# An AdaLN block of attention and a LoRA feed-forward layer: inputs turned on the host, LayerNorm on columns, the shift as a bias, and an instruction order of its own for each engine

## What is computed

```python
mod = (silu(c) @ wmod).reshape(B, 6, 1, H)           # c: 4 x 1024, wmod: 1024 x 6144
sa, ca, ga, sb, cb, gb = (mod[:, i] for i in range(6))
ga = (2 * (ga >= 0) - 1) * maximum(abs(ga), 0.25)     # gb the same
h = layernorm(x) * (1 + ca) + sa
q, k, v = split(h @ Wqkv + bqkv)                      # Wqkv: 1024 x 768
x = x + ga * (softmax(q @ k.T / 16) @ v @ Wo + bo)
h = layernorm(x) * (1 + cb) + sb
lora = (h @ A[adapter].T) @ Bw[adapter].T             # rank 16, an adapter for each batch, or none
x = x + gb * (h @ weight.T + bias + lora)             # weight: 1024 x 1024
```

## Time and profile before

| | |
|---|---|
| median of 3 runs | 1152.91 us (1152.84 to 1154.0) |
| the profiled execution's own time | 1153.4 us |
| its span, first to last instruction | 1151.6 us |
| mean granted clock of the matrix engine | 0.976 of full |
| busy, share of the span | PE 94%, PEld 78%, DVE 55%, ACT 33%, POOL 21% |
| moved by DMA | 160.26 MB, 139 GB/s over the span |

### The profile page before, as it was taken

How to read it: one execution, slowest core, us unless ns; L and a number is a source line. 1 busy time by engine, 2 the same in 40 slices (tenths; PEclk the granted TensorE clock), 3 DMA queues, 4 the chain that set the end, 5 groups by cost and what they waited for, 6 DMA issues and landing times.

```text
span 1151.6 us, 13779 instructions
## 1 busy us (share of the span) xinstructions
PE 1084.6 (94%) x5593; PEld 895.4 (78%) x5593; DVE 632.7 (55%) x837; ACT 381.0 (33%) x630; POOL 241.9 (21%) x211
## 2 busy tenths in 40 slices
PE   7799998999999999989999997999989999999996
PEld 2576997888987889878889875788777877787775
DVE  1830256463455462565625658737767776677631
ACT  0831144241343231542315443403422332323310
POOL 1000011231111221021401233233134122324122
PEclk9799999999998999999999998999999999999998
DMA  9975201533014340124310678543525462454221
GB/s 326 374 271 198 77 1 47 194 124 112 1 37 147 115 178 1 38 92 164 135 48 19 178 276 290 183 164 110 202 80 194 145 202 75 163 201 164 97 86 55
DMA packets 51968, 160.26 MB, mean 139 GB/s; under 512 B 5217, under 2 KB 9729, under 8 KB 51905
## 3 DMA queue, kind: packets, MB, share of 16 engines
q1 hardware_dynamic: 42208, 125.01, 31.4%
q0 software_dynamic: 9696, 34.36, 7.9%
HBM read 121.60 MB, written 37.75 MB: 138 GB/s over the span
## 4 chain that ended last, share of the span: by engine, by line
PE 64%; DVE 12%; issue 9%; DMA 6%; ACT 5%; POOL 3%; SPq 0%; DVEq 0%; POOLq 0%; ACTq 0%
PE pairA L1106 5%; PE pairB L1106 5%; PE pairA L1107 5%; PE pairC L1106 5%; PE pairA L1108 5%; PE pairB L1108 5%; PE pairB L1107 5%; PE pairC L1108 5%; PE pairC L1107 5%; PE pairD L1106 4%; PE pairD L1108 4%; PE pairD L1107 4%; ACT xs L770 2%; DVE w_sum L1065 2%; DVE bn L957 2%
## 5 line engine op out<-in xcount | busy, mean ns | idle before, releaser
L986 DVE TENSOR_TENSOR h_lo<-xs,h_hi 128x512 fp32r<-128x512 f32 x120 | 84.0, 741 | 91.3 <-ACT h_hi L778 91.0
L682 POOL TENSOR_TENSOR rstd<-mv,eps 128x2 f32<-128x2 f32 x32 | 9.1, 285 | 584.2 <-DVE mv L962 584.2
L957 DVE BATCH_NORM_STATS2 bn<-xs 128x6 f32<-128x512 f32 x120 | 75.3, 681 | 38.5 <-DMA xs<-x_dram 19.5
L1106 PE MATMUL pairA<-w_hi,h_hi 128*128 128x512 f32 x208 | 83.2, 400 | 11.2 <-issue 7.6
L978 DVE TENSOR_SCALAR xs<-xs,mv,rstd 128x1024 f32<-128x1024 f32 x60 | 82.7, 1420 | 18.6 <-POOL rstd L684 18.6
L703 POOL TENSOR_TENSOR res<-res,row_bc 128x1024 f32<-128x1024 f32 x32 | 80.1, 2518 | 24.4 <-ACT row_bc L734 14.5
L690 POOL TENSOR_TENSOR xr<-xr,row_bc 128x1024 f32<-128x1024 f32 x32 | 77.2, 2414 | 27.3 <-DMA xr<-in_L_attn_x 27.0
L848 ACT ACTIVATE w_hi<-w_sum 128x1024 fp32r<-128x1024 f32 x32 | 34.0, 1061 | 147.1 <-DVE w_sum L1065 147.0
L1107 PE MATMUL pairA<-w_lo,h_hi 128*128 128x512 f32 x208 | 82.0, 394 | 0.0
L1108 PE MATMUL pairA<-w_hi,h_lo 128*128 128x512 f32 x208 | 81.8, 393 | 0.0
L1106 PE MATMUL pairB<-w_hi,h_hi 128*128 128x512 f32 (+1 forms) x192 | 72.3, 376 | 0.0
(11 more groups left out here) (313 smaller groups left out, 2622.4 us busy)
## 6 DMA issues: line engine op xcount, KB each, us to landing
wm<-in_L_wmod SPq DMA_DIRECT2D x48, 512.0 KB, 7.0
xr<-in_L_attn_x SPq DMA_DIRECT2D x32, 512.0 KB, 3.6
x_dram<-xr POOLq DMA_DIRECT2D x32, 512.0 KB, 3.1
xs<-x_dram SPq DMA_DIRECT2D x32, 512.0 KB, 4.3
w2t<-w2t_dram SPq DMA_DIRECT2D x32, 512.0 KB, 4.5
res<-x_dram SPq DMA_DIRECT2D x32, 512.0 KB, 5.2
out_y<-res POOLq DMA_DIRECT2D x32, 512.0 KB, 3.4
xs<-in_L_attn_x SPq DMA_DIRECT2D x28, 512.0 KB, 5.0
```

Source lines behind the costliest of these rows:

```text
L957: nc.vector.bn_stats(bn[:, k, half, :], rows[:, k, half * BANK:(half + 1) * BANK]).then_inc(bn_made, 1)
L986: nc.vector.tensor_tensor(lo, h, hi.bitcast(F32), ALU.subtract).then_inc(h_lo_made, 1)
L1106: nc.tensor.matmul(out, left[0], right[0], start=first, stop=False)
```

## The change

The change rewrites most of the program.

- **Inputs from the host.** x is also given turned (x_cols, for each batch and chunk 128 x 8 x 512), Wqkv by part, the feed-forward weight turned, lora_B turned, c, bqkv, bo and bias as one small table of columns, and identity, selector and adapter numbers as one table.
- **LayerNorm of the first stage on columns.** The rows of x are still loaded, for statistics only (`LN`, `ST`). The eight statistics of a chunk of 512 rows (mean and reciprocal deviation of four tiles) are turned by one transpose (`RT0`), stored to DRAM and loaded spread over the partitions (`SW`, `LBC`). DVE subtracts the mean and multiplies by the reciprocal deviation on the turned x (`Z`, two tensor_tensor of 128 x 1024 for each of four parts), ACT rounds with the scale 1 + ca (`HH`), DVE forms the low part (`HL`). No transposes, no L770 in the first stage.
- **The shift as a bias.** sa is not added to h; its product with Wqkv (`SAW`, 48 small products of four columns, 96 instructions) is added to bqkv for each batch, and through `TWO` to the output's bias.
- **Modulation.** The scale's column comes first and directly as columns (`DC`: wmod stationary, c moving, 64 products of four columns, 128 instructions). The other five columns as before (`M`, `MT`).
- **Gate and bias vectors** are turned in three transposes (`RT`), stored to DRAM once, and loaded spread over the partitions (`LGA`, `LRA`, `LG2`, `LR2`).
- **Second stage.** LayerNorm on rows and T as before; ACT applies scale and shift within PSUM (`AF`), rounds 128 x 1024 from there, and DVE forms the low part from PSUM (`HL2`); the rows' buffer is free after the transposes, the PSUM pair after `HL2`.
- **Orders.** Each engine has a list of its own (PE_ORDER, ACT_ORDER, DVE_ORDER, SP_ORDER, POOL_ORDER), over the whole program. F runs by chunks of rows first and halves of the weight second.

The diff, cut to its core:

```diff
@@ the start of three of the new orders @@
+PE_ORDER = [
+    ("RT0", (0, 0), "A", None), ("DC", (0,), "B", None), ("DC", (1,), "B", None), ("DC", (2,), "B", None),
...
+    ("DC", (7,), "B", None), ("K", (0, 0, 0), "C", None), ("V", (0, 0, 0), "D", None), ("V", (0, 0, 1), "D", None),
+    ("RT0", (0, 1), "A", ("RT0", 0, 0)), ("M", (1, 0), "B", ("MT", 0)), ("Q", (0, 0, 0), "A", ("RT0", 0, 1)),
+    ("Q", (0, 0, 1), "A", None), ("M", (1, 1), "B", None), ("K", (0, 0, 1), "C", None),
+    ("MT", (1,), "D", ("V", 0, 0)), ("SAW", (), "B", ("M", 1)), ("M", (2, 0), "D", ("MT", 1)),
...
+DVE_ORDER = [
+    ("SI", (), None), ("ST", (0, 0), None), ("ST", (0, 1), None), ("ST", (0, 2), None), ("ST", (0, 3), None),
+    ("WQL", (1, 0), None), ("WQL", (1, 1), None), ("Z", (0, 0, 0), None), ("Z", (0, 0, 1), None),
+    ("Z", (0, 0, 2), None), ("Z", (0, 0, 3), None), ("MM", (0,), "B"), ("WQL", (2, 0), None),
+    ("HL", (0, 0, 0), None), ("HL", (0, 0, 1), None), ("HL", (0, 0, 2), None), ("HL", (0, 0, 3), None),
...
+SP_ORDER = [
+    ("Lsm",), ("Lid",), ("LN", 0, 0), ("LN", 0, 1), ("LN", 0, 2), ("LN", 0, 3), ("LWq", 1, 0), ("LWq", 1, 1),
+    ("LT", 0, 0, 0), ("LT", 0, 0, 1), ("LT", 0, 0, 2), ("LT", 0, 0, 3), ("Lwm", 0, 0), ("Lwm", 0, 1), ("Lwm", 0, 2),
...
@@ scalar engine @@
+                elif what == "SW":
+                    act.dma_start(stats_dram[q], stat_sb).then_inc(st_stat, 16)
+                elif what == "LBC":
+                    act.wait_ge(st_stat, 16 * (q + 1))
+                    src = stats_dram[q].rearrange("k n -> (k n)").partition_broadcast(P)
+                    act.dma_start(bc, src).then_inc(ld_bc, 16)
+                elif what == "HH":
+                    act.wait_ge(z_made, 8 * b + 4 * j + k + 1)
+                    act.wait_ge(mod_made, 1)
+                    for ct in range(2 * k, 2 * k + 2):
+                        nc.scalar.activation(h_hi[j][:, ct, :], z_cols[j][:, ct, :], ACT.Copy,
+                                             scale=modT[:, CA, b, ct:ct + 1]).then_inc(h0_hi_made, 1)
+                elif what == "AF":
+                    for cc in range(4):
+                        part = ps[:, cc * 2 * P:(cc + 1) * 2 * P]
+                        nc.scalar.activation(part, part, ACT.Identity, bias=modT[:, SB, b, ct:ct + 1],
+                                             scale=modT[:, CB, b, ct:ct + 1]).then_inc(h_affine, 1)
+                    nc.scalar.activation(h_tile(h_hi, n, half), ps[:, :].rearrange("p (c n) -> p c n", c=4),
+                                         ACT.Copy).then_inc(h_hi_made, 1)
@@ vector engine @@
+                elif what == "Z":
+                    dve.wait_ge(ld_cols[j][k], 16 * (b + 1))
+                    dve.wait_ge(ld_bc, 16 * (q + 1))
+                    nc.vector.tensor_tensor(z, z, mean, ALU.subtract).then_inc(z_centred, 1)
+                    dve.wait_ge(z_centred, 4 * q + k + 1)
+                    nc.vector.tensor_tensor(z, z, over, ALU.mult).then_inc(z_made, 1)
+                elif what == "HL2":
+                    nc.vector.tensor_tensor(h_tile(h_lo, n, half), ps[:, :].rearrange("p (c n) -> p c n", c=4),
+                                            h_tile(h_hi, n, half).bitcast(F32), ALU.subtract).then_inc(h_lo_made, 1)
@@ matrix engine @@
+                if what == "DC":
+                    pe.wait_ge(ld_wm[wm_slot(k)], 16)
+                    for ct in range(CT):
+                        last = nc.tensor.matmul(ps[:, ct * B:(ct + 1) * B], wm[wm_slot(k)][:, ct * P:(ct + 1) * P],
+                                                scT[:, k * B:(k + 1) * B], start=(k == 0 and ct == 0), stop=(k == CT - 1),
...
+                elif what == "SAW":
+                    for f in range(3 * DT):
+                        for k in range(CT):
+                            last = nc.tensor.matmul(ps[:, f * B:(f + 1) * B], w_raw[f // DT][:, k, f % DT * P:(f % DT + 1) * P],
+                                                    modT[:, SA, :, k], start=(k == 0), stop=(k == CT - 1))
+                elif what in ("Q", "K"):
+                        if b + j + m == 0 and what == "K":
+                            pe.wait_ge(h0_lo_made, ct + 1)
...
-                elif what == "gate":
-                    pe.wait_ge(gates_made, 2 * (b + 1) + 1)
-                    spread(ps, gate_col, gate_done)
...
-                elif what == "turn_w":
...
```

1421 lines of the change are left out of this document (700 added, 721 removed), and 445 rows, old and new, of tables (ACT_ORDER, ATTENTION, DVE_ORDER, END).

## The result

The changed kernel takes **1089.09 us** (median of four runs, 1085.82 to 1091.49) against 1152.88 us of the kernel before, a ratio of 0.9443 [0.9411, 0.9475]: 64 us faster. The forecast was 1105 us, the range 1079 to 1129; the sign and the range held, and the middle was 16 us too high. That distance is no single error: in the profile's span two terms were missed by 9 and 4 us on one side, and two by 25 and 10 on the other, so part of the nearness is luck.

What follows compares the result with a forecast made beforehand. The prediction took PE's instruction queue behind the first product as the bound, with the head and holes. Span: 1151.6 − 13.6 − 44.4 + 22.8 − 10.4 − 5 + 3 = 1104.0 us; forecast 1105, range 1079 to 1129.

Steps and rivals of the forecast that it cites:

- first product: Head: the first large product starts at 41 us instead of 54.6, 13.6 us gained.
- 51 blocks of transposes: Behind the first product: 51 blocks leave PE's queue at 0.87 us each, 44.4 us gained.
- added, with its clock: Behind the first product: modulation halves, turns and SAW add 22.8 us to PE, including 1.6 for SAW's clock.
- holes, with the new waits: PE's holes: 10.4 us less before PV, 5 less in the last attention, 3 more for new waits.
- The late-head rival: Head: statistics transfers of 12.6 us each give 1119 us, or slow DC gives 1123; chance 0.20.
- The charge for the clock: DC and SAW, long runs of small matmuls, each lose 1.6 us to a lowered clock.
- The 7.6 and 7.1 us at the feed-forward weights stay: Feed-forward part: PE's waits of 7.6 and 7.1 us stay, as DVE makes the same sums and low parts.
- the second stays and is late next: Last attention, 11.9 us of holes: waits from the pair of xr buffers stay; only 5 us come off.
- the first rival: Whole body: each engine's own order closes two thirds of the 23 us of holes kept, 1087 us; chance 0.22.
- The held pair of T: Second stage: PSUM pair waits for rounding and low part, up to 147 us over 32 blocks, 1252 us; chance 0.04.
- signs of error: PE idling over 25 us on statistics or unemptied pairs, first product after 48 us, DVE above 80% in feed-forward.
- signs of being right: K at 37 to 40 us, DC about 16, Z ending before DC, 456 transposes gone, first-to-last product 1054 us.

Runs made afterwards that it cites:

- the doubled ones: Changed kernel with the remaining transposes of the probabilities issued twice, 256 more: 1116.67 us, ratio 0.9673 to the kernel before.
- run with the wide column: Changed kernel with the first modulation column made by two wide product halves and eight turns instead of DC's 128 four-column instructions: 1077.32 us, ratio 0.9339.
- the maxima twice: Changed kernel with DVE taking the row maximum of each of the 32 score blocks twice: 1093.28 us, ratio 0.9468 to the kernel before.

## Why the prediction was right, and where it was wrong

The measured column is from the two profiles; the steps of PE are summed from each start to the next one's, without the waits, which are the holes.

| Term | forecast | measured | |
|---|---|---|---|
| first product | −13.6 | −4.2 | 54.62 to 50.41 |
| 51 blocks of transposes | −44.4 | −44.9 | 408 at 0.110; the doubled ones cost 0.109 each |
| added, with its clock | +22.8 | +26.7 | SAW 18.5 for 11.7, the others 8.2 for 11.1 |
| holes, with the new waits | −12.4 | −37.6 | 40.7 to 3.1 |
| behind the last product | 0 | +2.0 | 9.8 to 11.8 |
| the steps that stay, closer together | 0 | −9.6 | products 6.7, transposes of the probabilities 1.7, others 1.2 |
| span | −47.6 | −67.6 | 1151.6 to 1084.0 |

*The head: a rate mis-sized.* The steps before DC came as forecast: the first transfer of the statistics took 4.3 us (3.6 assumed), the second 6.8 (6.4), both over ACT's queue; the turn ran at 15.2 us (15), Z from 27.2 to 36.8 (25 to 35). (The rule of DMA: Bandwidth & Descriptors in the Trainium skill, Queues, rings and completion order, that each DMA engine serves its queues in turn, agrees: of the transfers issued by SP that landed between 14 and 30 us the median took 15.5 to 17.2 us from issue to landing, ACT's spread load 6.8 us.) Only DC's price was wrong: 0.214 us each, not 0.122. The late-head rival named this case, and against it I wrote that loading weights need not slow with the clock. The weight loads of DC and of the turns of the same shape (count, busy, mean ns) say that it does:

```profile
L1306 PEld LDWEIGHTS pairB<-scT,wm 128*128 128x128 f32 x128 | 27.4, 333 | 5.5 <-issue 5.5
...
L1327 PEld LDWEIGHTS pairD<-consts,row_bc 128*128 128x128 f32 x48 | 5.7, 192 | 0.2
```

With the rate right, the first product stands at 50 us. The run with the wide column shows it: 39.78 us, where the prediction had K at 39.3 to 41.

*The charge for the clock.* I charged 1.6 us behind each stretch of small matmuls (behind SAW the half column alone lost them, 3.66 us for 2.07) and went by the row against the rule of the Trainium skill (TensorE: Matmul & The Clock Gate, Part 1) that sustained activity releases the throttle. The row was right in sign: through 27 us of DC without a hole the clock did not rise, so this case's trace disagrees with the rule for matmuls of four columns. But the larger price is inside the stretch, 11.8 us in DC and 6.8 in SAW, and there I had charged nothing.

*The transposes: right only together with the order.* That PE's queue is the path, and so each removed block its 0.87 us, is true of the changed kernel as far as transposes put in show it (0.109 each; none was taken out there) and false of the kernel before (18.3 us taken out, 3.7 lost). The 44.9 us can't be credited to the removal as such.

*The holes: the failed step.* "The 7.6 and 7.1 us at the feed-forward weights stay" and "the second stays and is late next" were wrong; all of it went, as the first rival said. Its reason fits: from 742 us to the last product DVE is busy for some 249 of 399 us before and for 207.4 of 330 after, 0.62 and 0.63 of the time, and in the second no wait is over 1.2 us. Yet no run touched these waits alone, and the change altered the second stage's steps (where scale and shift are applied, what frees a pair) as well as its order. In the first stage the runs speak for the order from both sides: less work in the old order gave 2 of 7 us and −4 of 18; one place of the old order in the new kernel cost 6.4, another order in the old kernel 23; 39 us more work on DVE in the new order no more than some 4. That the new lists would close all holes with the *old* work wasn't tried; it would need the whole new list made for the old kernel.

*Closer products.* The products of 512 and 256 columns, equal in number, took 900.3 us before and 893.6 after. These 6.7 us are for the most part dips of the clock: by its record it is at half for 30.7 us between the first product and the last before, in places up to 6.8 us long, and after for 23.9, of which 20.5 are SAW and the half column behind it. I had counted one dip of some 1.6 us. The runs show that a hole can bring one, and not each time.

*The held pair of T* did not come: all waits ahead of a turn in the feed-forward part are 1.6 us together. Of my signs of error one came true, the first product after 48 us; the others (25 us on statistics or pairs, DVE over 80%) did not. Of the signs of being right the times in the head failed (K at 37 to 40 us, DC 16 us), and the stretch between first and last product is 1021.8 us, not 1054; Z did end before DC, and the clock was at half when K started and behind SAW. The 456 transposes are gone, and the others stand.

## What to carry to other kernels

Price a stretch of narrow matmuls at the clock that it will itself run at, and look for the form with the many columns as the moving operand: here that one step gave 11 and then 12 to 13 us. A matrix engine that is busy for 96% of a stretch isn't thereby its bound: take work out of its queue without making the other engines' lists anew, and the same waits end at the same time, and the clock can fall behind them. So cost a removal together with what comes late next at each place, and a new order by the holes that it can close: here the holes made 37.6 us, what was taken out less what was added 18.2.

## What the hardware showed that I had not expected

- A matmul of four columns in fp32 costs 0.107 to 0.122 us an instruction at 2.4 GHz and 0.213 at 1.2, and its weight load 192 and 333 ns. It follows the clock nearly as a wide product does (0.23 and 0.43).
- 128 such instructions without a hole left the clock at the lower level for 27 us; among V's products, at five of 256 columns to four small ones, it stayed there for 41 us and the V products with it. In the run with the wide column it rose 2.7 us into the first half and stayed up through 16 instructions of four columns.
- Two holes of 1.20 and 1.72 us with eight transposes between them left the clock of the first pass at 1.00 in one profile of the kernel before and took it to 0.50 for 3.4 us in another. Holes of 1.24 and 2.49 with one transpose between took it to 0.50 for 6.8 us in all three passes.
- One program does not repeat to the microsecond: the changed kernel ran 1085.8 to 1091.5 us, the kernel before 1150.8 to 1157.6 in the runs beside these experiments. In the changed kernel part of that is the length of its small stretches: SAW took 18.5, 20.5 and 18.0 us and Wo's turn 4.1, 4.0 and 7.0 in three profiles (the third is that of the maxima twice, which is alike up to there).
